# Loops of every engine at fixed instruction slots, with a hint for the back edge, in a Mamba-2 and mixture-of-experts layer

## The reference: what is computed

```python
xn = _layernorm(x, axis=-1)
x = x + _L0_attn_ref(xn, ...) + _L0_ffn_ref(xn, ...)
```

```python
weights_BTX, indices_BTX = jax.lax.top_k(probs_BTE, TOP_K)
norm_weights_BTX = jax.nn.softmax(weights_BTX, axis=-1)
...
fuse_BTEF = jax.nn.silu(gating_BTEF) * jnp.einsum('BTD,EDF->BTEF', x, kernel_up_EDF)
down_BTED = jnp.einsum('BTEF,EFD->BTED', fuse_BTEF, kernel_down_EFD)
```

## Time and profile before

| what | value |
|---|---|
| median of three runs | 802.36 us |
| lowest and highest run | 796.66 and 802.98 us |
| span of the profiled execution | 834.5 us |
| mean granted clock of TensorE | 0.950 |
| instructions recorded | 15563 |
| PE busy | 647.4 us, 78% |
| DVE busy | 594.7 us, 71% |
| ACT busy | 465.5 us, 56% |
| POOL busy | 456.1 us, 55% |

### The profile page before, as it was taken

How to read it: one execution, slowest core, us unless ns; L and a number is a source line. 1 busy time by engine, 2 the same in 40 slices (tenths; PEclk the granted TensorE clock), 3 DMA queues, 4 the chain that set the end, 5 groups by cost and what they waited for, 6 DMA issues and landing times. The chain is left out here.

```text
span 834.5 us, 15563 instructions
## 1 busy us (share of the span) xinstructions
PE 647.4 (78%) x3781; PEld 528.2 (63%) x3783; DVE 594.7 (71%) x1486; ACT 465.5 (56%) x966; POOL 456.1 (55%) x615
## 2 busy tenths in 40 slices
PE   0694538888998999888899897798888888889600
PEld 0694226667776777776676676677777777777500
DVE  7787978988888988888988887455555555555222
ACT  0441536587777777877778774455555555555300
POOL 3000017677777776777767776155555555555643
PEclk9999999999999999999999998899999999999855
DMA  9940100000000000000000024133232233323099
GB/s 308 275 111 0 28 1 24 19 25 25 25 24 20 24 24 20 28 21 23 21 24 21 27 97 114 43 91 93 88 95 85 88 95 90 95 82 93 24 265 338
DMA packets 72135, 62.53 MB, mean 75 GB/s; under 512 B 9544, under 2 KB 65231, under 8 KB 72112
## 3 DMA queue, kind: packets, MB, share of 16 engines
q1 hardware_dynamic: 63408, 45.19, 20.0%
q0 software_dynamic: 8704, 17.06, 5.9%
HBM read 30.73 MB, written 32.54 MB: 76 GB/s over the span
## 5 line engine op out<-in xcount | busy, mean ns | idle before, releaser
L440 POOL DMA_INDIRECT moe_d<-raw,slot_st x144 | 141.4, 982 | 132.6 <-issue 121.9
L414 POOL DMA_INDIRECT slots_d<-rows,slot_st x128 | 144.2, 1126 | 64.2 <-POOL rows L409 33.7
L997 DVE SCALAR_TENSOR_TENSOR act<-raw,taps,act 128x512 f32<-128x512 f32 x192 | 156.2, 821 | 12.4 <-ACT act L509 11.0
L394 POOL TENSOR_TENSOR xde<-xdt,e_end 128x256 f32<-128x256 f32 x64 | 43.8, 684 | 126.6 <-DVE xdt L1073 125.1
L848 PE MATMUL bank<-act,raw 128*128 x576 | 80.4, 283 | 28.1 <-ACT raw L635 25.6
L745 PE MATMUL bank<-xdt,m_sb 128*128 128x64 f32 x512 | 71.6, 284 | 38.3 <-DVE y_sb L1094 27.2
L1187 DVE CAST x_hi<-bank 128x256 fp32r<-128x256 f32 x72 | 30.6, 425 | 93.2 <-PE bank L831 52.8
L848 PEld LDWEIGHTS bank<-act,raw 128*128 128x128 f32 x576 | 70.7, 193 | 36.2 <-issue 36.2
L745 PEld LDWEIGHTS bank<-xdt,m_sb 128*128 128x128 f32 x512 | 63.7, 195 | 42.4 <-DVE y_sb L1094 29.9
L623 ACT ACTIVATE l_sb<-bank 128x256 f32<-128x256 f32 x144 | 47.3, 383 | 51.9 <-issue 26.5
L824 PE MATMUL bank<-xw_hi,x_hi 128*128 x144 | 63.8, 443 | 5.1 <-DVE x_lo L1189 4.4
(11 more groups left out here) (230 smaller groups left out, 1708.5 us busy)
## 6 DMA issues: line engine op xcount, KB each, us to landing
slots_d<-rows SPq DMA_DIRECT2D x8, 1188.0 KB, 13.2
rows<-slots_d SPq DMA_DIRECT2D x72, 132.0 KB
act<-moe_d SPq DMA_DIRECT2D x12, 512.0 KB, 7.3
x_sb<-in_x SPq DMA_DIRECT2D x8, 512.0 KB, 7.6
act<-in_x SPq DMA_DIRECT2D x64, 64.0 KB
out<-x_sb SPq DMA_DIRECT2D x8, 512.0 KB, 7.3
moe_d<-raw,slot_st POOLq DMA_INDIRECT x144
slots_d<-rows,slot_st POOLq DMA_INDIRECT x128
```

The source lines that it names most:

```text
L394: nc.gpsimd.tensor_tensor(by_head(xde[:, u, :]), by_head(xdt[:, u, :]), per_head(e_end, nn), ALU.mult).then_inc(xde_done, 1)
L414: nc.gpsimd.indirect_dma_start(out=slots_d, out_offset=bass.IndirectOffsetOnAxis(ap=slot_st[:, r, c:c + 1], axis=0), in_=rows[:, r, c, :], ...
L440: nc.gpsimd.indirect_dma_start(out=moe_d, out_offset=bass.IndirectOffsetOnAxis(ap=slot_st[:, r, c:c + 1], axis=0), in_=ym[r][:, c * D:(c + ...
L997: V.scalar_tensor_tensor(out=group_act(par)[:, t, :], in0=proj[:, t, k:k + GT], scalar=taps[:, t, k:k + 1], in1=group_act(par)[:, t, :], o ...
```

## The change

A helper `loop` takes the place of each engine's `Fori`. It is the same counted loop with two arguments more. [...] `hint_back_edge=True` puts one instruction, BRANCH_PREFETCH_HINT, at the top of the body. [...] All thirteen loops are changed: three each on PE, DVE and ACT, two each on POOL and SP. Nothing else is.

```diff
+        def loop(eng, start, end):
+            return nc.Fori(start, end, engines=bass.OrderedEngineSet([eng.engine]), hint_back_edge=True,
+                           head_slot={eng.engine: 0})
+
         def over_sequences(eng, body):
             body(0)
-            with eng.Fori(1, NB - 1) as b:
+            with loop(eng, 1, NB - 1) as b:
                 body(b)
             body(NB - 1)
...
             for m in range(TURN0):
                 turn(m, True)
-            with eng.Fori(TURN0, TURN1) as m:
+            with loop(eng, TURN0, TURN1) as m:
                 turn(m, False)
...
-            with act_e.Fori(1, NB) as it:
+            with loop(act_e, 1, NB) as it:
                 group(it)
...
-            with pe.Fori(1, NB) as it:
+            with loop(pe, 1, NB) as it:
                 turn_x(it, 0)
...
-            with dve.Fori(1, NB) as it:
+            with loop(dve, 1, NB) as it:
                 for u in range(2):
```

## The result

| | before | after |
|---|---|---|
| median of 12 runs each | 800.06 us | 810.03 us |
| lowest and highest | 796.18, 804.43 us | 804.63, 814.29 us |
| ratio | | 1.0112, 95% interval 1.0089 to 1.0135 |
| span of the profiled execution | 834.5 us | 809.1 us |

The change makes the kernel 1.1% slower. The two spans say the opposite of the two medians, and this is the first thing to settle: the profiled execution of before was not like the runs that are timed. The changed kernel's profile is, 809.1 us beside 810.91 for the run that it belongs to. That second profile is the one to compare with.

A forecast was written before the change was run, and what follows sets the result against it. PE's stream was taken as near the bound in all three loops, with handovers between engines the rest. Hint 1.5, jumps 0.6 and skipped blocks 0.5 gave +2.6 us on 802.4: 805.0 us, range 797 to 811.

The forecast's parts named there:

- term 1: The hint at the head of each turn, 29 on PE at 50 ns: +1.5 us, bounds 0 and 2.3.
- term 3: Code blocks skipped by the jumps at loop entries, mostly covered by waits: +0.5 us, bounds 0 and 3.6.
- rival C: Skipped blocks are paid at every loop entry, on PE and DVE too: 5.4 to 10.8 us, chance 0.12.
- term 4: Gain at the back edges: no fetch to save, 0; a quicker PE branch, 3.4 us, also taken as 0.
- Rival A: At PE's 26 taken back edges the branch gets quicker and the hint is hidden: 799 us, chance 0.08.
- Rival D: At the head of every turn the hint fetches held code, displacing a needed block: 35 to 47 us, chance 0.07.
- PE's loads run on through the branch from its queue: At PE's back edges queued loads keep the engine fed during the branch, so a quicker branch gains 0.
- The remark at the end of the prediction: In the third loop a changed handover between PE and ACT could turn 0.5 us into 8 us over 16 turns.
- the step from span to median: The whole profiled span, 834.5 us, is 32.1 us above the runs' median; this difference is carried over as it is.
- term 2: The jump at each loop entry, three on PE at 0.208 us: +0.6 us, lower bound 0.
- the cover that was named: At the first entry ACT waits 5.46 us for PE, which hides the arrival of code there.

The follow-up runs named there:

- hint_only: Changed kernel with the hints alone, no fixed head slots: ratio 1.0063 to before, +3.9 us at equal clock.
- before_again: The kernel before, unchanged, profiled a second time: ratio 1.0001, span 799.8 us.
- slot_near: Changed kernel without hints, head slots chosen per engine and loop to shorten the entry jumps: ratio 1.0030 to before, -0.1 us at equal clock.
- slot_only: Changed kernel with slot 0 at all heads, no hints: ratio 1.0043 to before, +2.1 us at equal clock.
- slot_third: Changed kernel without hints, slot 0 only for each engine's third loop: ratio 1.0009 to before, +0.3 us at equal clock.
- hint_pe_b: Changed kernel with hints in PE's three loops alone, no slots, where before takes 800 us: ratio 1.0080, +2.8 us at equal clock.
- hint_pe: Changed kernel with hints in PE's three loops alone, no slots, on a chip where before took 842.55 us: ratio 1.0003.

## Why the prediction was right or wrong

The time, 810.03 us, lies inside of the range, 797 to 811, at its edge. The forecast of 805.0, +2.6 us or 0.3%, was right in its sign and too small: measured is +10 us between the medians, 1.1% by the ratio. That the range holds the time is in part luck. It reached to 811 by the upper bounds of terms 1 and 3 and by rival C, whose condition did not come true on PE.

I gave a slowdown of over 1% a chance of 0.11, and that rested on a wrong sum: rival C with term 1 is 802.4 + 1.5 + 5.4 to 10.8 = 809 to 815, not 806 to 815. Most of it lies over 810.4, not a third, and the chance should have been near 0.17.

**No fetch at the back edges (term 4): right.** The loops' stretches have no instruction packet, before or after, and no gain came. What holds a body as long as that of PE's second loop ready no run shows. Rival A is out: PE's branch became slower, 220 for 208 ns, not quicker. Rival D is out: no fetches inside of the loops.

**The hint (term 1): mis-sized, 1.5 us for 3.9.** The hint's own row, 31 ns on PE, is below the 50 that I took. What failed is the step "PE's loads run on through the branch from its queue". In the first profile of before a load does start at 561.32 us, under the branch of 561.3, but no trace shows the queue, and in hint_only PE waits 0.08 to 0.13 us at the back edge. With that step fell the upper bound of 0.078 us a turn: at the third loop's back edge the hint costs 0.22 us a turn in all, seven times its row, through the gap before the next matmul and slower matmuls behind it. And it was not visible in the trace that I had, since there PE idled 11% of the third loop. The remark at the end of the prediction, that 16 turns multiply any shift of the handover, was nearer to it than the sum.

**The first profile (the step from span to median): wrong.** I carried 834.5 - 802.4 = 32.1 us over as a constant. It was 16 turns of the third loop at 2.4 us too much each, a rhythm in which PE has time to spare. "PE's stream comes near to being the bound" in rows 2 understated it: in before_again, whose span fits the timed runs, PE is busy without a gap in the third loop.

**The jump (term 2): right or less.** PE's jump takes 0.4 us, twice the 0.2 assumed, but slot_near, which has all the jumps, is at before's time within 0.4 us.

**The skipped blocks (term 3): a cost was there, mis-sized.** No run shows blocks of slots, or that a jump passes over one: the term was my estimate. What the runs show in its place are stalls, in the changed kernel of ACT at all three entries, of SP at both of its own, and of DVE and POOL at the third. 0.5 us was taken and slot_only costs 2.1, inside of the bound of 3.6. A stall took 2.4 to 3.1 us, not the 1.8 of one arrival, and 5.9 at the first entry, where the cover that was named held. The cover at the third (1.91 us on DVE, 2.50 on ACT) was read in the slower rhythm. ACT at the third entry in before_again, and after:

```profile
554.37 0.39 ACT L635 ACTIVATE raw<-bank 128x256 f32<-128x256 f32 x1 [0.30 <-PE bank L848]
...
561.83 0.38 ACT L639 ACTIVATE raw<-bank 128x256 f32<-128x256 f32 x1 [2.28 <-issue]
```

Only 0.30 us of idle time was there to cover the stall. After, ACT stands idle for 2.28 us and waits for its own issue, not for another engine. POOL had no share in the term, but in the changed kernel it stalls for 2.4 us, and queue 14 brings a packet meanwhile; in slot_only, with one instruction less in the body, it is 0.5 (566.4 to 566.9) with no instruction packet. The change's remainder, 7.2 - 3.9 - 2.1 = 1.2 us at equal clock, may be this; it wasn't tested, and with 0.4 us of error on each term it is not far from nothing. Of rival C this much holds: a stall is paid at some entries, but PE, with 0.4 us, has none.

**The clock.** Of the 10.0 us between the medians 7.2 are left at equal clock. The granted clock is 0.935 on average in the changed kernel's runs and 0.938 in the 93 runs of before that have one on record, which at 4.9 us for 0.01 is 1.3 us. Two means that differ by less than the spread of the runs (0.007) don't show that the change did it. The last 1.5 us lie in the 12 runs of before beside the result, which were a little faster than the other 93 and have no clock on record.

## What to carry to other kernels

Before costing anything from a profile, hold its span against the median of the plain runs, and if they differ by per cents, find the stage: divide the difference by the turns of each loop. On the engine that sets the pace, look at the work right behind the back edge: if it is slower there than elsewhere in the turn (1.61 against 1.40 us here), try the loop's cut at another place of the same order, behind work that is already handed over and away from register loads. Here a loop without instruction packets gained nothing from an aligned head; if one is wanted, try other slots (ACT's third entry took 3.1 us with slot 0 at all heads and 0.2 us with the slots of slot_near) and look for instruction packets at the entry.

## What the runs showed of the hardware that was not expected

- The forward jumps in whose course queue 14 brings a packet (about 8 KB, 0.20 MB in 24) stop the sequencer of ACT, DVE, SP or POOL for 2.4 to 3.1 us at the third entry of the changed kernel and at that of slot_only. At the first entry ACT's takes 5.9 us in both while the input is loaded. The jumps at the third entry in whose course no such packet comes take 0.2 to 0.6 (slot_near, slot_third, POOL in slot_only, PE in all).
- With a hint in the body PE's taken branch takes 216 ns instead of 208 at the second and third loop (hint_pe_b), 226 and 220 in the changed kernel. The place matters too: slot_near, without hints, has 215 at the third.
- One program, that of hint_pe and hint_pe_b, runs its third loop in 12.2 us a turn on one chip and in 14.1 to 14.5 on another. The kernel before takes 800 against 842 us there, at nearly the same granted clock (0.941 against 0.934 on average).
- The run-to-run scatter of this kernel, 792 to 809 us, goes with TensorE's granted clock: of a standard deviation of 3.9 us, 1.3 remain at equal clock.
